# Metaformer block on one core: VectorE's order at a group's scales, and weight loads one per convolution group

## Chip, cores and metric

One core of one Trainium2 chip. The metric is the device time of a run in microseconds; a run is compared by the median.

## What is computed

```python
def reference(x, conv_weight, W1, b1, W2, b2):       # x: (16, 192, 32, 32)
    w_sym = mean of the four rotations of conv_weight (7 x 7, depthwise)
    x = x + dwconv(ln_c(x), w_sym)                   # ln_c: over the channels, eps 1e-6
    t = x as (16, 1024, 192)
    h = quantize(ln_t(t) @ sign(W1 - mean).T + b1)   # 768 hidden, groupwise
    out = quantize(gelu(h) @ sign(W2 - mean).T + b2)
    return t + out
# 5 groups of 3 images: gamma = max|group|; quantize = clip(y * 128 / (gamma + 1e-5)); image 16 keeps t alone
```

The quantisation needs the largest magnitude of a whole group of three images before any of its elements can go on, twice: once before the GELU, once before the output.

## The kernel before

**Convolution.** 48 groups of 4 channels (`conv_group`, L976) are products of TensorE with band matrices. Each group's band is fetched by four DMAs of 112 KB (`load_bands`, L296), two on SyncE's and two on ScalarE's queue, into three buffers up to group 25 and four from group 26 on (`BUFS`). A buffer is free when the group that used it last is done, so a band's fetch begins when the group three (later four) before it is done. VectorE adds each group's result to x (L750, one per group). POOL clears the fourth buffer (L406) once group 23 is done (`ROOM[FOURTH]`) and then, once 24 groups are done, starts ten DMAs that load the weights of the two linear layers: W1 (L409) and W2 (L411), five each, of 115 KB. VectorE reads them at groups 28 to 32 (`weight_sums`), and the signs and transposes of the weights follow. The region that they land in is part of the normalised input of the convolution, so it is free only once the groups that read it are done.

**Tokens.** An item is a half image, 512 tokens; there are 30 with a feed-forward part (`FT`), in groups of 6 (`GT`). The loop runs over steps s, and every engine has the instructions of several items in a step, in an order that is written out: hidden products for item s, GELU for s - 6 (`LAGA`), f16 high part and cast for s - 7 (`LAGH`), second products (`lower`, `upper`) for s - 8, largest output for s - 9, output for s - 15 (`LAGF`). f32 values go to TensorE as an f16 high part and an f16 remainder ("low part").

TensorE in a step: for each of six blocks of 128 hidden channels the products of item s (L1026 to L1028) and those of item s - 8 (L1058); after block 1 the transposes of tokens s + 1 (L1012, L1015), which need their normalisation; after block 4 the transposes of x for the output (`x_back`, L999 to L1004), which need the output of the item before (`fin`); at the end the upper products (L1068). The first product of step s + 1 needs the tokens' low parts.

VectorE in a step: `normal(s + 2)` (L816, four instructions), `high` (cast, L831), `final` (output, L897 and L898), `largest(s - 1)` (L844, of 3072 columns), `token_low(s + 1)` (L822, L824), `largest2` (L870). POOL has most of the hidden low parts (L435); from item 23 (`LAST`) VectorE has some of them (`low`, L839).

A group's scale: VectorE reduces the largest over the group (L847), TensorE turns it to a row (`as_row`, L1033), VectorE takes the row's maximum (`over_row`, L851), TensorE sends it to all partitions (`to_all`, L1038), VectorE works out the scale (`scale`, L856 to L866). This is at steps 6, 12, ..., 30 (`first`). The second scale (L879 to L887, `scale2`) does the same at steps 15, 21, ..., 39 (`first2`). There `to_all` on TensorE stands behind the transposes of tokens.

SyncE in a step fetches parked x (L341) for `normal`, and stores the output of item s - 16 (L348) once it is done; one queue does both in order.

## Time and profile before

| | |
|---|---|
| median of 3 runs | 613.7 us (611.32 to 615.29) |
| profiled execution, its time | 617.74 us |
| its span | 615.9 us |
| mean granted clock of TensorE | 0.918 |
| TensorE, VectorE, ScalarE, POOL busy | 81%, 76%, 62%, 36% |

The profile is of one execution; times are us from the start of its span, and L numbers are lines of the kernel before. Convolution runs from 88 to 235 us, tokens from there to the end. Idle time of an engine counts only where another one waits for it.

### The profile page before, as it was taken

The page shows a single profiled execution, that of the slowest core. Times are in us where ns is not written, and L with a number is a line of the kernel's source. Part 1 is how long each engine was busy: PE and PEld are TensorE (multiplying, and loading weights), DVE is VectorE, ACT ScalarE, POOL GpSimd, SP SyncE. Part 2 cuts the span into 40 slices and gives each one's busy share as a digit, 9 for nine tenths or more (in the row PEclk, how much of TensorE's full clock was granted, in tenths as well). Part 3 has the DMA queues.
Part 4 walks back from the last instruction along what each step waited for, and adds up shares of the span by engine and source line. Part 5 has one row for each costly group of instructions (what it writes and reads, how often), then busy time and mean ns, then how long its engine had stood idle before and what let it go on. Part 6 is the DMA issues. An engine that isn't in the chain of part 4 may idle for free.

```text
span 615.9 us, 9847 instructions
## 1 busy us (share of the span) xinstructions
PE 496.8 (81%) x3552; PEld 353.5 (57%) x3552; DVE 467.1 (76%) x1041; ACT 382.0 (62%) x598; POOL 219.7 (36%) x221
## 2 busy tenths in 40 slices
PE   2355527999969996758789989998999999987893
PEld 2255527999969995324335545555555555545562
DVE  7987861222228987996799898799989989699675
ACT  2688950000000353637799989998999898989550
POOL 4000000000400002212076747576666567558450
PEclk9666759999979997979999989999999999999798
DMA  8998325566965646940011000122222423263345
GB/s 223 290 316 248 104 61 150 149 175 169 204 161 150 178 124 250 386 157 1 27 51 53 27 27 0 52 82 74 78 74 77 133 78 101 80 230 104 125 135 178
DMA packets 55280, 81.29 MB, mean 132 GB/s; under 512 B 7361, under 2 KB 39105, under 8 KB 55232
## 3 DMA queue, kind: packets, MB, share of 16 engines
q1 hardware_dynamic: 39616, 68.28, 36.5%
q10 hardware_dynamic: 15136, 11.22, 6.5%
q0 software_dynamic: 480, 1.17, 0.9%
q8 instruction: 28, 0.46, 0.3%
q14 instruction: 20, 0.16, 0.1%
HBM read 53.12 MB, written 27.53 MB: 131 GB/s over the span
## 4 chain that ended last, share of the span: by engine, by line
PE 42%; DVE 22%; ACT 18%; DMA 10%; issue 5%; SPq 3%; ACTq 0%; DVEq 0%
PE bank L976 19%; DMA arena<-x 6%; PE bank L1058 5%; ACT arena L566 5%; DVE am L844 5%; ACT arena L560 4%; DMA arena<-kz_d 3%; PE bank L1026 3%; PE bank L1027 3%; PE bank L1028 3%; PE bank L1068 2%; DVE arena L816 2%; DVE arena L831 2%; ACT arena L482 2%; DVE arena L766 2%
## 5 line engine op out<-in xcount | busy, mean ns | idle before, releaser
L435 POOL TENSOR_TENSOR arena<-arena 128x512 f16<-128x512 f32 x159 | 186.9, 1212 | 120.6 <-DVE arena L831 99.3
L976 PE MATMUL bank<-arena 128*128 128x112 f32 (+1 forms) x1152 | 136.1, 283 | 20.8 <-ACT arena L482 12.6
L560 ACT ACTIVATE arena<-bank,b1s 128x512 f32<-128x512 f32 x180 | 125.1, 703 | 42.2 <-PE bank L1028 41.8
L976 PEld LDWEIGHTS bank<-arena 128*128 128x128 f32 x1152 | 135.0, 199 | 21.7 <-ACT arena L482 12.8
L1058 PE MATMUL bank<-arena 128*128 128x512 f16 x360 | 106.4, 390 | 5.4 <-ACT arena L584 3.6
L566 ACT ACTIVATE arena<-arena,gm 128x1024 f32<-128x1024 f32 x90 | 102.7, 1163 | 1.7 <-DVE gm L866 1.7
L844 DVE TENSOR_REDUCE am<-arena 128x1 f32<-128x3072 f32 x30 | 100.3, 3343 | 3.5 <-ACT arena L560 3.5
L750 DVE TENSOR_TENSOR arena<-bank,arena 128x512 f32<-128x512 f32 x48 | 33.2, 691 | 81.0 <-PE bank L976 80.9
L1026 PE MATMUL bank<-arena 128*128 128x512 f16 x180 | 71.0, 395 | 26.0 <-DVE arena L824 17.7
L497 ACT ACTIVATE arena<-arena,wmean 51x576 f16<-51x576 f32 (+1 forms) x10 | 8.6, 856 | 129.0 <-DVE wmean L724 116.2
L1027 PE MATMUL bank<-arena 128*128 128x512 f16 x180 | 70.6, 392 | 0.0
L1028 PE MATMUL bank<-arena 128*128 128x512 f16 x180 | 70.2, 390 | 0.0
L958 PE MATMUL bank<-identf,arena 128*128 128x128 f32 x128 | 33.4, 365 | 40.9 <-DMA arena<-x 40.9
L1058 PEld LDWEIGHTS bank<-arena 128*128 128x128 f16 x360 | 34.5, 99 | 47.7 <-issue 4.6
L426 POOL TENSOR_SCALAR arena<-arena,VR,SM 128x192 f32<-128x192 f32 x28 | 14.4, 526 | 108.8 <-DVE arena L816 75.7
L816 DVE TENSOR_SCALAR arena<-arena,VR,SM 128x192 f32<-128x192 f32 x92 | 44.1, 539 | 8.4 <-issue 8.2
L1026 PEld LDWEIGHTS bank<-arena 128*128 128x128 f16 x180 | 17.8, 99 | 56.6 <-DVE arena L824 21.3
L958 PEld LDWEIGHTS bank<-identf,arena 128*128 128x128 f32 x128 | 22.7, 194 | 42.8 <-DMA arena<-x 32.6
L831 DVE CAST arena<-arena 128x2048 f16<-128x2048 f32 (+1 forms) x30 | 35.8, 1195 | 13.6 <-ACT arena L566 11.9
L1068 PE MATMUL bank<-arena 128*64 128x256 f16 x720 | 46.1, 276 | 0.0
L1068 PEld LDWEIGHTS bank<-arena 128*64 128x64 f16 x720 | 37.5, 109 | 13.8 <-issue 13.4
L573 ACT ACTIVATE arena<-arena 128x1024 f16<-128x1024 f32 x37 | 39.7, 1072 | 1.7 <-PE bank L1068 1.7
(118 smaller groups left out, 684.9 us busy)
## 6 DMA issues: line engine op xcount, KB each, us to landing
arena<-park_d SPq DMA_DIRECT2D x44, 384.0 KB, 3.6
arena<-kz_d SPq DMA_DIRECT2D x100, 112.0 KB, 2.9
arena<-kz_d ACTq DMA_DIRECT2D x92, 112.0 KB, 3.4
park_d<-arena SPq DMA_DIRECT2D x6, 1536.0 KB, 14.5
arena<-x SPq DMA_DIRECT2D x8, 1024.0 KB, 8.9
out<-arena SPq DMA_DIRECT2D x32, 256.0 KB, 2.0
kz_d<-arena SPq DMA_DIRECT2D x8, 672.0 KB, 11.0
arena<-x SPq DMA_DIRECT2D x16, 256.0 KB, 9.8
```

The source lines that it names most:

```text
L435: last = pool.tensor_tensor(out=low_half(u, m, m + 1), in0=yslot(u)[:, 2 * m:2 * m + 2, :], in1=hib(u, m, m + 1), op=ALU.subtract)
L560: act.activation(yslot(s)[:, 2 * m:2 * m + 2, :], m1p[c % 2][:, :].rearrange("p (h n) -> p h n", h=2), ACT.Identity, bias=b1s[:, m:m + 1], ...
L566: act.activation(y, y, ACT.Gelu, scale=gm[:, 5:6]).then_inc(gelu, 1)
L816: last = v.tensor_scalar(TN[:, h % 2, jj, :], x1[:, jj, :], VR[:, n:n + 1], SM[:, n:n + 1], ALU.mult, ALU.add)
L844: v.tensor_reduce(am[:, u % GT:u % GT + 1], yslot(u), AX.XY, ALU.max, apply_absolute_value=True).then_inc(amx, 1)
L958: t.transpose(o[:, b, 0:P], nat[k % 2][:, b, cols], identf[:, :])
L976: last = t.matmul(ps[:, :, lo:hi], WB[BUFS[g]][:, 1 - db, c, :], xn[:, :, lo + db:hi + db], start=(db == 0), stop=(db == -1))
L1026: t.matmul(o, W1A[:, fs], TT[:, s % 2, 0, :], start=True, stop=False)
L1027: t.matmul(o, W1M[:, fs], TT[:, s % 2, 1, :], start=False, stop=False)
L1028: t.matmul(o, W1Q[:, fs], TT[:, s % 2, 2, :], start=False, stop=True).then_inc(mm1, 1)
L1058: last = t.matmul(o, W2T[:, m, 0:P], src, start=(i == n == 0), stop=(i == MT - 1 and n == 1))
L1068: last = t.matmul(m2b[e * C1:(e + 1) * C1, 0:QTR], W2T[:, m, P:C], src[:, e, :], start=(m == n == 0), stop=(m == MT - 1 and n == 1))
```

## The change

The weight loads go out one at a time: W1's five when 12, 13, ..., 16 convolution groups are done (`ROOM_W`), W2's five at 17 to 21, ahead of the clearing of the fourth buffer. Two assertions state that the region is free by then.

On VectorE: at steps 6, 12, 18 and 24 `token_low` comes directly behind `scale`, ahead of `normal`. At steps 15, 21 and 27 `over_row` comes ahead of `high`, and `scale2` and `final` ahead of `largest`. At step 33 `over_row` comes ahead of the cast, and `scale2` and `final` ahead of the low parts. All other steps keep their order, and no instruction is added or taken out.

```diff
+ROOM_W = (12, 17)
...
             pool.wait_ge(conv, ROOM[THIRD])
             pool.memset(WF[2], 0.0).then_inc(blank, 1)
+            for q in range(GROUPS):
+                pool.wait_ge(conv, ROOM_W[0] + q)
+                pool.dma_start(w1w[0:RP1, q, :], w1[q * 3 * RP1:(q + 1) * 3 * RP1, :]
+                               .rearrange("(p r) c -> p (r c)", r=3)).then_inc(ld_w, 16)
+            for q in range(GROUPS):
+                pool.wait_ge(conv, ROOM_W[1] + q)
+                pool.dma_start(w2w[0:RP2, q, :], w2[q * RP2:(q + 1) * RP2, :]).then_inc(ld_w, 16)
             pool.wait_ge(conv, ROOM[FOURTH])
             pool.memset(WF[3], 0.0).then_inc(blank, 1)
-            pool.wait_ge(conv, ROOM[FOURTH] + 1)
-            for q in range(GROUPS):
-                pool.dma_start(w1w[0:RP1, q, :], w1[q * 3 * RP1:(q + 1) * 3 * RP1, :]
-                               .rearrange("(p r) c -> p (r c)", r=3)).then_inc(ld_w, 16)
-                pool.dma_start(w2w[0:RP2, q, :], w2[q * RP2:(q + 1) * RP2, :]).then_inc(ld_w, 16)
...
-                if u >= LAST:
-                    dve.wait_ge(hiV, u + 1)
-                    low(u, HL, MT)
-                    dve.wait_ge(hiA, u + 1)
-                    low(u, LP, HL)
+                if u == LAST:
+                    lows_here(u)
...
+                if s <= FT:
+                    if first:
+                        if 0 <= s - LAGF < FT:
+                            final(s - LAGF)
+                        largest(s - 1)
+                        over_row(0, g)
+                        if s == FT:
+                            scale(g)
+                        if 0 <= s - LAGH < FT:
+                            high(s - LAGH)
+                        if s < FT:
+                            scale(g)
+                            token_low(s + 1)
+                    if s > 5 and s + 2 < FT:
+                        normal(s + 2)
+                    if first2:
+                        over_row(1, g2)
+                    if not first and 0 <= s - LAGH < FT:
+                        high(s - LAGH)
+                    if first2:
+                        scale2(g2)
+                    if not first and 0 <= s - LAGF < FT:
+                        final(s - LAGF)
+                    if not first and 1 <= s:
+                        largest(s - 1)
+                    if not first and 0 <= s + 1 < FT:
+                        token_low(s + 1)
+                else:
+                    if first2:
+                        over_row(1, g2)
+                    elif 0 <= s - LAGF < FT:
+                        final(s - LAGF)
                     if 0 <= s - LAGH < FT:
                         high(s - LAGH)
...
+                    if first2:
+                        scale2(g2)
+                        final(s - LAGF)
+                    if 0 <= s - LAGH < FT:
+                        lows_here(s - LAGH)
```

The order of VectorE's instructions at step 12, from a group's scale on, before (`arena` holds all big tiles, `gm` the scales, `bank` is PSUM):

```order
L866 TENSOR_SCALAR gm<-gm 128x1 [waits gelu,gsc_t]
L816 TENSOR_SCALAR arena<-arena,VR,SM 128x192 [waits trQ,ld_l2,nm]
L816 TENSOR_SCALAR arena<-arena,VR,SM 128x192 x3
L822 TENSOR_TENSOR arena<-bank,arena 128x512 [waits thi]
L824 TENSOR_TENSOR arena<-bank,arena 64x512 [waits tlo]
L870 TENSOR_REDUCE am<-arena 128x1 [waits ev2]
```

and after:

```order
L874 TENSOR_SCALAR gm<-gm 128x1 [waits gelu,gsc_t]
L827 TENSOR_TENSOR arena<-bank,arena 128x512 [waits thi]
L829 TENSOR_TENSOR arena<-bank,arena 64x512 [waits tlo]
L821 TENSOR_SCALAR arena<-arena,VR,SM 128x192 [waits trQ,ld_l2,nm]
L821 TENSOR_SCALAR arena<-arena,VR,SM 128x192 x3
L878 TENSOR_REDUCE am<-arena 128x1 [waits ev2]
```

The two low-part instructions, which take a bank and write 512 columns, have moved ahead of the four of the normalisation (128x192).

VectorE at step 15, before, from the cast on:

```order
L831 CAST arena<-arena 128x2048 [waits mm2b,gelu]
L851 TENSOR_REDUCE gs<-bank 1x1 [waits gtr1]
L844 TENSOR_REDUCE am<-arena 128x1 [waits ev1]
L879 TENSOR_SCALAR gm<-bank 128x1 [waits gall2]
L880 RECIPROCAL gm<-bank 128x1
L882 RECIPROCAL gm<-gm 128x1 [waits gsc2_t]
L884 TENSOR_SCALAR gm<-gm 128x1 [waits gsc2_t]
L887 TENSOR_SCALAR gm<-gm 128x1 [waits gsc2_t]
L897 SCALAR_TENSOR_TENSOR arena<-arena,gm,bank 128x512 [waits xps,gsc2]
L898 SCALAR_TENSOR_TENSOR arena<-arena,gm,bank 128x256
L822 TENSOR_TENSOR arena<-bank,arena 128x512 [waits thi]
L824 TENSOR_TENSOR arena<-bank,arena 64x512 [waits tlo]
```

and after:

```order
L859 TENSOR_REDUCE gs<-bank 1x1 [waits gtr1]
L836 CAST arena<-arena 128x2048 [waits mm2b,gelu]
L887 TENSOR_SCALAR gm<-bank 128x1 [waits gall2]
L888 RECIPROCAL gm<-bank 128x1
L890 RECIPROCAL gm<-gm 128x1 [waits gsc2_t]
L892 TENSOR_SCALAR gm<-gm 128x1 [waits gsc2_t]
L895 TENSOR_SCALAR gm<-gm 128x1 [waits gsc2_t]
L905 SCALAR_TENSOR_TENSOR arena<-arena,gm,bank 128x512 [waits xps,gsc2]
L906 SCALAR_TENSOR_TENSOR arena<-arena,gm,bank 128x256
L852 TENSOR_REDUCE am<-arena 128x1 [waits ev1]
L827 TENSOR_TENSOR arena<-bank,arena 128x512 [waits thi]
L829 TENSOR_TENSOR arena<-bank,arena 64x512 [waits tlo]
```

The row's maximum (`gs<-bank`) is now ahead of the cast, and the second scale and the output (128x512 and 128x256, which write `arena` from `gm` and `bank`) are ahead of the maximum of 3072 columns (`am<-arena`).

VectorE at step 33, before, from the cast on:

```order
L831 CAST arena<-arena 128x1024 [waits mm2b,gelu]
L839 TENSOR_TENSOR arena<-arena 128x1024 [waits hiV]
L839 TENSOR_TENSOR arena<-arena 128x512 [waits hiA]
L851 TENSOR_REDUCE gs<-bank 1x1 [waits gtr1]
L879 TENSOR_SCALAR gm<-bank 128x1 [waits gall2]
L880 RECIPROCAL gm<-bank 128x1
L882 RECIPROCAL gm<-gm 128x1 [waits gsc2_t]
L884 TENSOR_SCALAR gm<-gm 128x1 [waits gsc2_t]
L887 TENSOR_SCALAR gm<-gm 128x1 [waits gsc2_t]
L897 SCALAR_TENSOR_TENSOR arena<-arena,gm,bank 128x512 [waits xps,gsc2]
L898 SCALAR_TENSOR_TENSOR arena<-arena,gm,bank 128x256
L870 TENSOR_REDUCE am<-arena 128x1 [waits ev2]
```

and after:

```order
L859 TENSOR_REDUCE gs<-bank 1x1 [waits gtr1]
L836 CAST arena<-arena 128x1024 [waits mm2b,gelu]
L887 TENSOR_SCALAR gm<-bank 128x1 [waits gall2]
L888 RECIPROCAL gm<-bank 128x1
L890 RECIPROCAL gm<-gm 128x1 [waits gsc2_t]
L892 TENSOR_SCALAR gm<-gm 128x1 [waits gsc2_t]
L895 TENSOR_SCALAR gm<-gm 128x1 [waits gsc2_t]
L905 SCALAR_TENSOR_TENSOR arena<-arena,gm,bank 128x512 [waits xps,gsc2]
L906 SCALAR_TENSOR_TENSOR arena<-arena,gm,bank 128x256
L847 TENSOR_TENSOR arena<-arena 128x1024 [waits hiV]
L847 TENSOR_TENSOR arena<-arena 128x512 [waits hiA]
L878 TENSOR_REDUCE am<-arena 128x1 [waits ev2]
```

The low parts (128x1024 and 128x512) have moved from behind the cast to behind the output.

## Rows read from the trace of the kernel before

**Rows 1.** The page's first part: busy time and share of span

```profile
PE 496.8 (81%) x3552; PEld 353.5 (57%) x3552; DVE 467.1 (76%) x1041; ACT 382.0 (62%) x598; POOL 219.7 (36%) x221
```

**Rows 2.** Waits of TensorE, 357 to 560 us: total, times, longest

```profile
PE bank L1026 <- DVE arena L824: 5.6, 3, 2.4
PE bank L1033 <- DVE gm L847: 2.2, 2, 1.4
PE bank L999 <- DVE arena L898: 1.7, 2, 0.9
PE bank L999 <- issue: 1.4, 1, 1.4
```

**Rows 3.** Windows: length, busy PE, PEld, DVE, ACT, POOL; clock, DMA share, GB/s

```profile
120.00:136.00 16.00, 16.00 (x146) 16.00 (x145) 4.07 (x7) 0.00 (x0) 0.00 (x0) 1.00 0.64 172
...
168.00:176.00 8.00, 3.09 (x25) 2.97 (x26) 1.36 (x2) 0.00 (x0) 0.00 (x0) 0.87 1.02 219
176.00:184.00 8.00, 8.00 (x52) 8.00 (x53) 2.40 (x4) 0.00 (x0) 0.00 (x0) 0.70 0.36 109
```

**Rows 4.** Timeline of VectorE (start us, length us): additions of groups 26, 28, 29

```profile
167.98 0.69 DVE L750 TENSOR_TENSOR arena<-bank,arena 128x512 f32<-128x512 f32 x1 [1.99 <-PE bank L976]
...
181.12 0.69 DVE L750 TENSOR_TENSOR arena<-bank,arena 128x512 f32<-128x512 f32 x1 [9.22 <-PE bank L976]
...
183.80 0.69 DVE L750 TENSOR_TENSOR arena<-bank,arena 128x512 f32<-128x512 f32 x1 [0.48 <-PE bank L976]
```

**Rows 5.** Chain of waits, 155 to 200 us

```profile
163.25 12.42 DMA arena<-kz_d
```

**Rows 6.** DMA queues, 150 to 190 us: packets, MB, share

```profile
q0 software_dynamic: 480, 1.17, 14.2%
```

**Rows 7.** DMA issues, 104 to 158 us: count, KB, us to landing

```profile
arena<-kz_d ACTq DMA_DIRECT2D x39, 112.0 KB, 3.1
arena<-kz_d SPq DMA_DIRECT2D x38, 112.0 KB, 2.9
```

**Rows 8.** The same, 158 to 165 and 163 to 170 us

```profile
arena<-kz_d ACTq DMA_DIRECT2D x7, 112.0 KB, 5.4
...
arena<-kz_d SPq DMA_DIRECT2D x6, 112.0 KB, 8.4
```

**Rows 9.** Timeline of VectorE, step 12: normalisation

```profile
360.14 3.99 DVE L816 TENSOR_SCALAR arena<-arena,VR,SM 128x192 f32<-128x192 f32 x4
```

**Rows 10.** Timeline of TensorE, end of step 12, start of 13

```profile
361.53 1.53 PE L1068 MATMUL bank<-arena 128*64 128x256 f16 x24
365.50 0.61 PE L1026 MATMUL bank<-arena 128*128 128x512 f16 x1 [2.44 <-DVE arena L824]
```

**Rows 11.** Timeline of ScalarE, the same place

```profile
362.35 3.22 ACT L566 ACTIVATE arena<-arena,gm 128x1024 f32<-128x1024 f32 x3
367.00 0.69 ACT L560 ACTIVATE arena<-bank,b1s 128x512 f32<-128x512 f32 x1 [1.43 <-PE bank L1028]
```

**Rows 12.** Timeline of VectorE, steps 15 and 16

```profile
388.78 3.33 DVE L844 TENSOR_REDUCE am<-arena 128x1 f32<-128x3072 f32 x1
...
399.14 1.25 DVE L816 TENSOR_SCALAR arena<-arena,VR,SM 128x192 f32<-128x192 f32 x4 [2.98 <-issue]
```

**Rows 13.** Timeline of TensorE, step 15: the broadcast

```profile
389.51 0.38 PE L1038 MATMUL bank<-gs,arena 1*128 1x1 f32 x2
```

**Rows 14.** Windows, as rows 3, around step 24

```profile
486.00:496.00 10.00, 8.43 (x64) 5.11 (x63) 9.86 (x18) 8.27 (x13) 6.82 (x6) 1.00 0.10 40
```

**Rows 15.** Timeline of VectorE, step 26

```profile
504.22 1.25 DVE L816 TENSOR_SCALAR arena<-arena,VR,SM 128x192 f32<-128x192 f32 x4 [1.54 <-issue]
```

**Rows 16.** Timeline of VectorE, step 33: low parts

```profile
567.18 2.91 DVE L839 TENSOR_TENSOR arena<-arena 128x1024 f16<-128x1024 f32 x2
```

**Rows 17.** Timeline of TensorE, step 33

```profile
570.31 0.58 PE L1038 MATMUL bank<-gs,arena 1*128 1x1 f32 x2 [3.01 <-DVE gs L851]
```

**Rows 18.** Windows, as rows 3, end of step 33

```profile
570.30:578.00 7.70, 7.69 (x43) 4.68 (x44) 3.87 (x10) 1.00 (x3) 1.89 (x2) 0.58 0.39 128
```

More of the change, by code:

```diff
@@ L131, in build @@
         assert at + GROUPS * HID <= XB + 6 * BLK
+        assert XB + WW + WTN + GROUPS * 3 * C <= XB + ROOM_W[0] * NN * CG
+        assert all(at + (q + 1) * HID <= XB + (ROOM_W[1] + q) * NN * CG for q in range(GROUPS))
         w1s = [w1w[:, g, 0:3 * C // 2].bitcast(F16).rearrange("p (r c) -> p r c", r=3) for g in range(GROUPS)]
@@ L831, in high, with lows_here @@
                 v.tensor_copy(hib(u, ha(u), MT), yslot(u)[:, 2 * ha(u):2 * MT, :]).then_inc(hiV, 1)
-                if u >= LAST:
-                    dve.wait_ge(hiV, u + 1)
-                    low(u, HL, MT)
-                    dve.wait_ge(hiA, u + 1)
-                    low(u, LP, HL)
+                if u == LAST:
+                    lows_here(u)
+            def lows_here(u):
+                dve.wait_ge(hiV, u + 1)
+                low(u, HL, MT)
+                dve.wait_ge(hiA, u + 1)
+                low(u, LP, HL)
             def low(u, m0, m1):
@@ L907, in _ @@
                 first, first2 = s % GT == 0 and 1 <= g <= FT // GT, (s - LAGF) % GT == 0 and 0 <= s - LAGF < FT
-                if first:
-                    if 0 <= s - LAGF < FT:
-                        final(s - LAGF)
-                    largest(s - 1)
-                    over_row(0, g)
-                    if s == FT:
-                        scale(g)
+                if s <= FT:
[20 more added lines that the diff above has]
+                    if not first and 0 <= s - LAGF < FT:
+                        final(s - LAGF)
+                    if not first and 1 <= s:
[7 more added lines that the diff above has]
+                        final(s - LAGF)
@@ L915, in _ @@
                     if 0 <= s - LAGH < FT:
                         high(s - LAGH)
-                    if s < FT:
-                        scale(g)
-                if s > FT and not first2 and 0 <= s - LAGF < FT:
-                    final(s - LAGF)
-                if s > 5 and s + 2 < FT:
-                    normal(s + 2)
-                if not first and 0 <= s - LAGH < FT:
-                    high(s - LAGH)
-                if first2:
-                    over_row(1, g2)
-                elif not first and s <= FT and 0 <= s - LAGF < FT:
-                    final(s - LAGF)
@@ L929, in _ @@
-                if not first and 1 <= s <= FT:
-                    largest(s - 1)
-                if first2:
-                    scale2(g2)
-                    final(s - LAGF)
-                if 0 <= s + 1 < FT:
-                    token_low(s + 1)
+                    if first2:
[3 more added lines that the diff above has]
+                        lows_here(s - LAGH)
                 for k in range(len(BATCH)):
```

## Prediction

> **What bounds the kernel now.** I read five views. The page's first part [rows 1] gives TensorE 496.8 of 615.9 us: the busiest engine, idle or slowed for only a fifth. So the question is where it is held, and whether that is where the change acts. The waits of TensorE in the token stage [rows 2] are short and few: three for the tokens' low parts (5.6 us), two for a group's maximum (2.2), three for an output that VectorE has not finished (1.7 and 1.4). The stretches of the convolution [rows 3] show a full engine at clock 1.00 from 120 to 136 us, 3.09 busy of 8 between 168 and 176, and then a full engine at 0.70. VectorE's additions, one per convolution group, mark the pace [rows 4], the chain of waits names what was late [rows 5], and the DMA views say why [rows 6 to 8].
>
> The profiled execution took 617.74 us, 615.9 of span and 1.8 around it. The median of the runs is 613.7, 4.0 lower. I sum against the profiled one and take the saving in us off the median.
>
> **Weight loads, one per convolution group.** Before, ten loads went out within 5 us, behind group 24. They are 1.17 MB and took 14.2% of 16 engines over 40 us [rows 6], which is 5.7 us of all engines. The bands that the convolution needs take 0.64 of the engines at full pace [rows 3], so 0.36 is free and the burst needs 5.7/0.36 = 16 us to drain. From 160 us that gives 176, and group 28's band did land at 175.7, 12.4 us after it was issued [rows 5]. The additions of groups 26 and 29 are at 167.98 and 183.80 [rows 4]: 15.8 us for three groups. A group takes 2.68 at the steady pace (2.0 of idle and 0.69 of work before each addition), so three are 8.0, and 7.8 us are lost. Of these 4.9 are idle time of TensorE between 168 and 176, the other 2.9 the clock at 0.70 behind it [rows 3]. (The Trainium skill, TensorE: Matmul & The Clock Gate, Part 1, has the clock halved when the array idles and calls the ramp less than 1% of a typical span. Left out for that, this term would be 4.9 and the whole sum 16.2; the row at 0.70 decides for counting it.)
>
> After, a load goes out at each of groups 12 to 21. One load is a tenth, 0.57 us of all engines, in a group's 2.68 x 0.36 = 0.96 us of free time, so nothing piles up. What hides it: with three buffers a band may be issued when the group three before it is done, and is needed two groups later, 5.4 us. Its second DMA goes out some 0.7 us late and lands 3.1 us after issue [rows 7], leaving about 1.6. A load that costs each band 0.6 us fits; if the cover is gone, each of ten groups pays. On POOL the clearing of the fourth buffer now stands behind the loads, but the last load waits for group 21 and the clearing for 23, and the sums that read the weights come at group 28. Bounds of the term: 0 (the lateness moves, below) to 7.8; I take 7.8. Since TensorE runs the convolution to its end and everything behind starts from there, this shifts all that follows.
>
> **Low parts directly behind a scale (steps 6, 12, 18, 24).** VectorE's normalisation of a later half took 3.99 us at step 12 and stood ahead of the two low-part instructions; TensorE waited 2.44 for them [rows 9, 10]. Now they run from 360.1 to about 361.5, and TensorE, done with the step before at 363.0 (361.53 + 1.5), goes on at once. The normalisation then ends at 365.5; the transposes that need it come about 2.2 us into TensorE's step, at 365.2, so it just covers. ScalarE is in its three GELU pieces until 365.5 [rows 11], where before it had to wait until 367.0 for TensorE: it gains 1.5 at once. Above the gap lies what the slow clock behind it cost: the product at 365.50 took 0.61 us, and some 3 us went at half speed, at most 1.4 of them for nothing. Bounds 1.5 and 3.8; I take the gap, 2.4. At step 6, which lies before the stretch of rows 2, I take 0: ScalarE has its GELUs in one piece there and no slack behind them. At steps 18 and 24 the other 5.6 - 2.4 = 3.2 us go.
>
> **Second scale and output ahead of cast and maximum (steps 15, 21, 27).** The maximum alone is 3.33 us [rows 12]. The output of the first half of a group came behind it, and TensorE waited 1.7 + 1.4 us for it in all [rows 2]. It now comes about 2.3 us sooner: 3.3 less some 0.9 in which VectorE waits for TensorE's broadcast, which is behind a transposition of tokens, ends at 389.9 and was hidden by the maximum [rows 13]. There is a second effect: SyncE stores an output before it fetches the next parked tokens, so the normalisation at 399.14 sat idle for 2.98 us [rows 12]. It comes about 1.9 sooner, and with it the next maximum, for which TensorE waited 0.8 at step 18 (one of the two of 2.2 us; the other is at step 30 and stays).
>
> Together steps 15 to 27 can give 3.2 + 0.8 + 3.1 = 7.1. I don't take it all. VectorE was busy 9.86 of 10 us around step 24, TensorE 8.43 [rows 14]: once TensorE's waits are gone, VectorE's lateness is next. The maximum now stands ahead of the low parts, which come about 1 us later in these three steps, where my dates leave 0 to 0.6; and a fetch that made VectorE wait 1.54 at step 26 [rows 15] is not moved. I charge 0.5 at step 21 and 1 and 0.7 at steps 24 to 27: 4.9 stay. Bounds 0 and 7.1.
>
> **The end (step 33).** Low parts of VectorE (567.18, 2.91 us) stand ahead of the row maximum, and TensorE waits 3.01 for it and then runs 570.3 to 578.0 at clock 0.58 [rows 16 to 18]. Now the row maximum comes first, at 567, then cast, scale and output to 569.9; low parts end at 572.8. TensorE's next transposition waits for the output, 569.9, so its step ends near 573.3 and not 577.8: 4.5 us. VectorE gains less: output and cast of step 34 come behind the low parts, 3.0 us sooner than before. ScalarE waits for TensorE's product, not for VectorE, and gains the 4.5; it sets the pace of the steps that follow, so VectorE catches up in part. Bounds 3.0 and 4.5; I take 4.0.
>
> **Sum.** 7.8 + 2.4 + 4.9 + 4.0 = 19.1 us. The profiled execution would be 598.6, the median 613.7 - 19.1 = 594.6; I say 595. Edits that cost nothing: the number of instructions and their shapes are the same on every engine.
>
> **Rivals.**
> VectorE takes over: steps 15 to 27 give nothing, the end 3.0. For it: its 9.86 of 10 us busy [rows 14] and the later low parts. Against it: VectorE's idle 2.98 goes at the same time. 7.8 + 2.4 + 3.0 = 13.2, 600.5 us.
>
> The lateness moves: each load delays a band by more than the 1.6 us of cover. For it: landing was already 5.4 us on ScalarE's queue while the burst began [rows 8], which would be 0.7 late, 7 us in ten groups, and 602; I put the case at half that, 0.5 each, 599.7. Against it: that row has several loads in flight, and later there is one at a time. (The Trainium skill, DMA: Bandwidth & Descriptors, Queues, rings and completion order, has each engine take turns between queues by packet; by that a band waits for its share of a single load, which agrees with 0.57, but it should also have spared group 28, which landed 12.4 us late, so I lean on the rows.)
>
> Both together: 613.7 - 2.4 - 3.0 - 0.3 = 608, within 1%.
>
> Slower: bands land during a load as they did at the height of the burst, 8.4 us after issue on SyncE's queue [rows 8]. Place: groups 12 to 22. Price: 8.4 - 3.1 - 1.6 = 3.7 us for each of ten, 37 - 19.1 = 18 more, 631.6 us. It decides from 1.9 us each, a landing of 6.6 us. Against it: this needs a backlog of several us, and each load leaves 0.4 us of free time behind it.
>
> More than forecast: all waits go, 7.8 + 3.8 + 7.1 + 4.5 = 23.2, 590.5.
>
> **How the numbers follow.** Forecast 0.60 (its own range 591 to 599), VectorE takes over 0.16, lateness moves 0.12, both 0.05, slower 0.04, more 0.03. Faster by over 1% (about what a measurement of this kernel can tell from no change) is 0.60 + 0.16 + 0.12 + 0.03 = 0.91, within it 0.05, slower 0.04. The range goes from all waits, 589, to both middle rivals with some to spare, 604.
>
> **What would show it.** Right: additions 2.68 us apart through groups 26 to 29, no clock below 1.00 there, band landings under 4.5 us at groups 12 to 22; no wait of TensorE for the low parts at steps 12, 18 and 24; the 3.01 us wait gone and clock near 1.00 at step 33. Wrong: waits of TensorE for band DMAs between groups 12 and 24 (second rival, or the slower one), or new waits for the low parts at steps 16, 22 and 28 that sum to over 2.2 us (first rival).

## The result and the profile after

| | median, range, runs |
|---|---|
| before, beside it | 613.16 us (611.32 to 615.29), 4 |
| after | 598.44 us (598.03 to 598.90), 4 |
| ratio after/before | 0.9719 [0.9681, 0.9758] |

The change saves 14.7 us by these medians, where 19 were forecast; 598.4 lies in the range of 589 to 604. The ratio on record, 0.9719, is not that of the two medians (0.976, which lies just outside its interval); it stands for 17.2 us. A second comparison of the same two kernels (`e5_after`, below) gave 17.7 us by medians and 18.9 by its ratio, 0.9693 [0.9643, 0.9743]. So the size is known to some 4 us, 15 to 19. One run of `e4_end`, of 616.08 us, fell into a slower state of the chip and is left out of its times. The profiled execution of after took 598.64 us, the one of before 617.74: 19.1 us apart, which is the sum of the prediction to the tenth. That agreement is partly luck, as the experiments show: two terms were too large and two too small, and the profile of before happened to be long in two places.

The page of after: span, busy time, and the group of VectorE's normalisation.

```profile
span 596.8 us, 9847 instructions
PE 492.4 (83%) x3552; PEld 350.2 (59%) x3552; DVE 463.5 (78%) x1041; ACT 380.4 (64%) x598; POOL 218.8 (37%) x221
L821 DVE TENSOR_SCALAR arena<-arena,VR,SM 128x192 f32<-128x192 f32 x92 | 44.1, 539 | 1.8 <-issue 1.6
```

TensorE is still the busiest engine; its busy time fell by 4.4 us though it runs the same 3552 instructions, because less of it runs at the low clock. VectorE's normalisation has an idle time of 1.8 us ahead of it; before it was 8.4.

**The convolution.** Stretches of after (columns as in [rows 3]: busy time and count of PE, PEld, DVE, ACT, POOL, then granted clock, DMA share, GB/s). The first four answer to [rows 3], the next two are the start of the token stage, the last two answer to [rows 14] and [rows 18].

```profile
120.00:136.00 16.00, 15.62 (x140) 15.47 (x139) 3.92 (x6) 0.00 (x0) 1.75 (x3) 1.00 0.67 178
136.00:152.00 16.00, 15.81 (x142) 15.66 (x142) 4.15 (x6) 0.00 (x0) 3.09 (x6) 1.00 0.83 208
168.00:176.00 8.00, 8.00 (x74) 8.00 (x74) 2.99 (x5) 0.00 (x0) 0.00 (x0) 1.00 0.65 176
176.00:184.00 8.00, 8.00 (x74) 8.00 (x73) 6.57 (x10) 0.00 (x0) 0.00 (x0) 1.00 0.65 171
233.00:239.00 6.00, 3.27 (x17) 2.82 (x18) 3.06 (x10) 2.50 (x6) 3.89 (x8) 0.59 1.02 392
239.00:245.00 6.00, 6.00 (x20) 3.14 (x18) 5.35 (x40) 1.81 (x3) 1.52 (x3) 0.56 1.03 398
476.00:486.00 10.00, 9.38 (x68) 5.35 (x67) 9.97 (x15) 8.72 (x14) 7.80 (x8) 1.00 0.01 5
549.50:557.80 8.30, 7.38 (x73) 4.75 (x73) 6.76 (x16) 7.70 (x10) 6.41 (x5) 1.00 0.18 52
```

From 168 to 184 TensorE is full at 1.00, where before it had 3.09 of 8 and then 0.70. VectorE's additions keep 2.68 us apart through groups 26 to 29, where [rows 4] had 15.8 us for three:

```profile
169.03 0.69 DVE L755 TENSOR_TENSOR arena<-bank,arena 128x512 f32<-128x512 f32 x1 [1.99 <-PE bank L995]
171.71 0.69 DVE L755 TENSOR_TENSOR arena<-bank,arena 128x512 f32<-128x512 f32 x1 [1.99 <-PE bank L995]
174.39 0.69 DVE L755 TENSOR_TENSOR arena<-bank,arena 128x512 f32<-128x512 f32 x1 [1.99 <-PE bank L995]
177.07 0.69 DVE L755 TENSOR_TENSOR arena<-bank,arena 128x512 f32<-128x512 f32 x1 [0.48 <-PE bank L995]
```

But the stretch from 120 to 152, full before, now has two small waits for bands, of 0.38 and 0.19 us; TensorE's timeline there (start, us, count; idle before it and what ended it):

```profile
114.15 13.62 PE L995 MATMUL bank<-arena 128*128 128x128 f32 x120 [0.36 <-DMA arena<-kz_d]
128.15 16.30 PE L995 MATMUL bank<-arena 128*128 128x128 f32 x144 [0.38 <-DMA arena<-kz_d]
144.65 43.10 PE L995 MATMUL bank<-arena 128*128 128x128 f32 x384 [0.19 <-DMA arena<-kz_d]
```

DMA issues of after from 128 to 155 us (count, KB each, median us to landing), for [rows 7]; five loads of W1 and five of W2 fall here:

```profile
arena<-kz_d SPq DMA_DIRECT2D x20, 112.0 KB, 3.3
arena<-kz_d ACTq DMA_DIRECT2D x20, 112.0 KB, 3.9
arena<-w POOLq DMA_DIRECT2D x5, 114.8 KB, 3.2
arena<-w POOLq DMA_DIRECT2D x5, 114.0 KB, 3.3
```

Bands land 3.3 us after issue on SyncE's queue and 3.9 on ScalarE's, where [rows 7] had 2.9 and 3.1: later by 0.4 and 0.8 us, less than the 1.6 us of cover. The wait of 0.38 us ends at 128.15, when the first of the ten loads is only being issued, and four of the five profiles with the loads behind group 24 have such a wait at the same group, of 0.38 to 0.56 us; that of 0.19 falls among the loads.

**The token stage.** TensorE's waits from 340 to 545 us, against [rows 2]. The 5.6 us for the low parts (L824 before, L829 now) and the 1.7 for an output (L898, now L906) have no row any more; of the two for a maximum (L847, now L855) the one at step 30 is left. New, but for one wait of 0.2 us in before, is the first row, for ScalarE's eviction of the hidden products:

```profile
PE bank L1045 <- ACT arena L565: 1.8, 4, 0.6
PE bank L1052 <- DVE gm L855: 1.4, 1, 1.4
```

Step 12 on VectorE, for [rows 9]: low parts first, normalisation behind them.

```profile
354.82 0.68 DVE L827 TENSOR_TENSOR arena<-bank,arena 128x512 f16<-128x512 f32 x1
355.54 0.68 DVE L829 TENSOR_TENSOR arena<-bank,arena 64x512 f16<-64x512 f32 x1
```

And on TensorE, for [rows 10]: the next step's first product at 357.67 waits for nothing, and the transposes of tokens behind the normalisation are not late. Two small waits are left in the step, 0.25 us for POOL and, behind the rows shown, 0.36 for ScalarE.

```profile
356.21 1.53 PE L1087 MATMUL bank<-arena 128*64 128x256 f16 x24
357.67 0.39 PE L1045 MATMUL bank<-arena 128*128 128x512 f16 x1
...
358.75 0.61 PE L1077 MATMUL bank<-arena 128*128 128x512 f16 x2 [0.25 <-POOL arena L440]
```

Step 15 on VectorE, for [rows 12]: TensorE's broadcast comes out uncovered by 0.72 us, the output is done before the maximum, and the normalisation has no idle time, where it had 2.98.

```profile
381.66 0.16 DVE L887 TENSOR_SCALAR gm<-bank 128x1 f32<-128x1 f32 x1 [0.72 <-PE bank L1057]
...
382.49 0.75 DVE L905 SCALAR_TENSOR_TENSOR arena<-arena,gm,bank 128x512 f32<-128x512 f32 x1
...
383.54 3.35 DVE L852 TENSOR_REDUCE am<-arena 128x1 f32<-128x3072 f32 x1
...
388.99 1.23 DVE L821 TENSOR_SCALAR arena<-arena,VR,SM 128x192 f32<-128x192 f32 x4
```

Step 33 on TensorE, for [rows 17 and 18]: the broadcast (L1057) waits for nothing, and the clock stays at 1.00 (last row of the stretches above). One step later a new wait stands, 1.49 us for the fetch of parked x.

```profile
552.34 0.38 PE L1057 MATMUL bank<-gs,arena 1*128 1x1 f32 x2
...
554.87 0.63 PE L1018 MATMUL bank<-identf,arena 128*128 128x128 f32 x4 [0.72 <-issue]
...
561.62 0.63 PE L1018 MATMUL bank<-identf,arena 128*128 128x128 f32 x4 [1.49 <-DMA arena<-park_d]
```

**Where the span's 19.1 us went in this pair.** Taking the start of each step's last upper products (L1068, now L1087) in both traces, after is ahead by 5.3 us up to step 12, 8.3 at 13, 9.3 at 15, 11.0 at 19, 12.0 at 21, 12.7 at 25, 14.3 at 27, 14.0 at 31, 19.8 at 33, 18.4 at 34, 19.3 at the end. So the convolution brought 5.3 (7.8 forecast; 0.6 of the 5.3 was there before its first product), step 12 3.0 (2.4), steps 15 to 27 6.0 (4.9), step 33 5.8 less the 1.4 of the new wait, of which 1.2 comes back a step later (4.0).

### The profile page after: what moved, and what is told of

Read it like the earlier page. It is cut to its first block, busy times and chain, and to the rows that moved or that the text cites. A ratio compares the mean times of both kernels' runs of the same rounds, so it can differ in the third digit from the quotient of the medians.

```text
span 596.8 us, 9847 instructions
## 1 busy us (share of the span) xinstructions
PE 492.4 (83%) x3552; PEld 350.2 (59%) x3552; DVE 463.5 (78%) x1041; ACT 380.4 (64%) x598; POOL 218.8 (37%) x221
## 4 chain that ended last, share of the span: by engine, by line
PE 52%; ACT 19%; DVE 12%; DMA 10%; issue 4%; SPq 1%; ACTq 0%; DVEq 0%
PE bank L995 18%; PE bank L1077 8%; ACT arena L571 5%; DMA arena<-x 5%; ACT arena L565 5%; PE bank L1045 5%; PE bank L1087 4%; PE bank L1047 4%; PE bank L1046 4%; DMA arena<-kz_d 4%; DVE am L852 3%; ACT arena L487 2%; ACT arena L578 2%; DVE arena L771 2%; PE bank L977 2%
## 5 line engine op out<-in xcount | busy, mean ns | idle before, releaser
L995 PE MATMUL bank<-arena 128*128 128x112 f32 (+1 forms) x1152 | 133.8, 279 | 20.4 <-ACT arena L487 16.0
L565 ACT ACTIVATE arena<-bank,b1s 128x512 f32<-128x512 f32 x180 | 125.0, 705 | 36.2 <-PE bank L1047 35.9
L995 PEld LDWEIGHTS bank<-arena 128*128 128x128 f32 x1152 | 132.5, 196 | 21.5 <-ACT arena L487 16.2
L1087 PE MATMUL bank<-arena 128*64 128x256 f16 x720 | 46.1, 276 | 0.0
L1087 PEld LDWEIGHTS bank<-arena 128*64 128x64 f16 x720 | 37.5, 109 | 13.8 <-issue 13.4
L836 DVE CAST arena<-arena 128x2048 f16<-128x2048 f32 (+1 forms) x30 | 34.5, 1149 | 7.9 <-ACT arena L571 7.1
```

Of the source, the lines that this page charges most:

```text
L565: act.activation(yslot(s)[:, 2 * m:2 * m + 2, :], m1p[c % 2][:, :].rearrange("p (h n) -> p h n", h=2), ACT.Identity, bias=b1s[:, m:m + 1], ...
L995: last = t.matmul(ps[:, :, lo:hi], WB[BUFS[g]][:, 1 - db, c, :], xn[:, :, lo + db:hi + db], start=(db == 0), stop=(db == -1))
L1087: last = t.matmul(m2b[e * C1:(e + 1) * C1, 0:QTR], W2T[:, m, P:C], src[:, e, :], start=(m == n == 0), stop=(m == MT - 1 and n == 1))
```

## The experiments

The theory was the prediction's: four gains that add up. The rivals were VectorE's lateness in the token stage and late bands in the convolution.

### Each part alone

Four kernels, each the kernel before with one part of the change, beside 21 runs of before (614.17 us, 609.50 to 617.95).

**The weight loads alone** (`e1_weights`):

```diff
+ROOM_W = (12, 17)
...
-            pool.wait_ge(conv, ROOM[FOURTH])
-            pool.memset(WF[3], 0.0).then_inc(blank, 1)
-            pool.wait_ge(conv, ROOM[FOURTH] + 1)
             for q in range(GROUPS):
+                pool.wait_ge(conv, ROOM_W[0] + q)
                 ...                         # W1's load q
+            for q in range(GROUPS):
+                pool.wait_ge(conv, ROOM_W[1] + q)
                 ...                         # W2's load q
+            pool.wait_ge(conv, ROOM[FOURTH])
+            pool.memset(WF[3], 0.0).then_inc(blank, 1)
```

> The kernel before with the weight loads moved alone, one per convolution group from 12 on. Theory (the burst made the gap of groups 26 to 29, and it closes): additions 2.68 us apart through groups 26 to 29, three or four small waits for bands of 0.2 to 0.4 us between groups 12 and 20, the convolution ends 6 to 7 us sooner, and the median falls by 6 us (4.5 to 7.5). Rival (the profiled execution of before had a longer gap than its other runs): the profile shows the same closed gap, but the median falls by 1.5 to 4 us only.

Measured 607.80 us (606.74 to 611.73), ratio 0.9897 [0.9864, 0.9930]: 6.4 us, as expected. TensorE's timeline has 30 groups, the fifth to the 34th, in one row:

```profile
102.84 80.94 PE L979 MATMUL bank<-arena 128*128 128x128 f32 x720 [1.48 <-DMA arena<-kz_d]
```

Behind its first 1.48 us no band is late in this execution, so ten spread loads need not cause a wait. (In other profiles small ones stand among them, see the lengths below.)

**Low parts behind the scale alone**, steps 6, 12, 18 and 24 (`e2_lows`):

```diff
                     if s < FT:
                         scale(g)
+                        token_low(s + 1)
...
-                if 0 <= s + 1 < FT:
+                if not first and 0 <= s + 1 < FT:
                     token_low(s + 1)
```

> The kernel before with the tokens' low parts directly behind the scale at steps 6, 12, 18 and 24 alone. Theory (TensorE's three waits for L824 are on the path): the wait of 2.44 at step 12 and the two of 1.57 go, the median falls by 4 us (2.4 at step 12 and about 0.8 each at 18 and 24, where VectorE is late next). Rival (VectorE's lateness returns at the outputs of steps 15, 21, 27, whose waits of 0.87, 0.87 and 1.43 grow by what was gained): the median falls by 2.4 or less.

Measured 610.38 us (606.18 to 613.80), 0.9936 [0.9902, 0.9970]: 3.8 us. TensorE's waits from 355 to 560 us:

```profile
PE bank L1000 <- DVE arena L898: 2.1, 2, 1.2
PE bank L1027 <- ACT arena L560: 1.8, 4, 0.6
```

The three waits for low parts are gone. In their place stand the waits for ScalarE's evictions (L560), seen in the whole change too, and the wait for the output at step 15 grew from 0.87 to 1.23 us. By steps: +3.0 at step 12, -0.4 at 15, -0.4 at 18, +0.7 at 19, +0.7 at 25, -0.3 at 27. Those at 18 and 27 prove nothing: `e1_weights`, unchanged there, has -0.6 and -0.2. The 0.4 at step 15 does not stand in it, so the rival, VectorE's lateness coming back at the outputs, holds in that small part.

**Second scale and output first alone**, steps 15, 21 and 27 (`e3_scale2`):

```diff
+                early2 = first2 and s < FT
+                if early2:
+                    over_row(1, g2)
                 if not first and 0 <= s - LAGH < FT:
                     high(s - LAGH)
-                if first2:
+                if early2:
+                    scale2(g2)
+                    final(s - LAGF)
+                elif first2:
                     over_row(1, g2)
...
-                if first2:
+                if first2 and not early2:
                     scale2(g2)
                     final(s - LAGF)
```

> The kernel before with the second scale and the output ahead of cast and maximum at steps 15, 21 and 27 alone (row maximum ahead of the cast, output ahead of the 3.3 us maximum). Theory: the three waits for the output (0.87, 0.87, 1.43) and the 0.81 for the maximum at step 18 go, the idle 2.98 of VectorE at step 16 shrinks to under 1.2, the median falls by 4 us (3 to 5). Rival (the low parts, now behind the maximum, are late): waits of TensorE for the low parts appear at steps 16, 22 and 28, and the median falls by under 2.

Measured 610.69 us (606.36 to 611.61), 0.9947 [0.9917, 0.9977]: 3.5 us. Waits of TensorE, 355 to 555 us:

```profile
PE bank L1032 <- DVE arena L824: 5.6, 3, 2.4
PE bank L1039 <- DVE gm L847: 1.4, 1, 1.4
```

The 5.6 us are those of before, in the same three places. The low parts that now come behind the maximum at steps 15, 21 and 27 are not late for TensorE. By steps: 1.06 at 15, 0.96 at 18, 1.06 at 21, 1.67 at 27, together 4.8 us, more than the medians give but inside their interval (1.4 to 5.1).

**Step 33 alone** (`e4_end`):

```diff
+                if s == 33:
+                    over_row(1, g2)
                 if not first and 0 <= s - LAGH < FT:
                     high(s - LAGH)              # without its low parts at s == 33
-                if first2:
+                if first2 and s != 33:
                     over_row(1, g2)
...
                 if first2:
                     scale2(g2)
                     final(s - LAGF)
+                if s == 33:
+                    lows_here(26)
```

> The kernel before with the second scale and the output ahead of the low parts at step 33 alone. Theory (a TensorE wait of 3.01 us and the half clock behind it): the wait goes, clock above 0.9 in that step, the median falls by 4.5 us (3.5 to 5.5). Rival (only the wait counts, and VectorE's later low parts take the rest): 2 to 3 us.

Measured 610.69 us (606.06 to 613.05), 0.9941 [0.9913, 0.9968]: 3.5 us, at the lower end of what was expected. The broadcast no longer waits, and the step looks as in the whole change:

```profile
564.58 0.38 PE L1045 MATMUL bank<-gs,arena 1*128 1x1 f32 x2
...
567.11 0.63 PE L1006 MATMUL bank<-identf,arena 128*128 128x128 f32 x4 [0.72 <-issue]
```

The four savings are 6.4 + 3.8 + 3.5 + 3.5 = 17.2 us, each known to some 2 us. They add up to what the whole brings (14.7 to 18.9), within some 4 us: no large part of one gain is another's.

### The whole again, and its neighbours

Four kernels, beside 11 runs of before (614.57 us, 610.71 to 619.32).

**The whole change, unchanged** (`e5_after`):

> The changed kernel once more, beside the next three on the same chip. Theory (the profiled execution of before was 3 to 4 us longer than its median by chance, in the clock behind step 33 and in the loads of x): the changed kernel is 15.5 us (14.5 to 17) under before's median here, and its runs differ by little. Rival (the 19.1 of the two spans is the true size): 18 us or more.

Measured 596.89 us (593.31 to 598.41, 6 runs), 0.9693 [0.9643, 0.9743]: 17.7 us, above the 14.5 to 17 that were expected and just under the 18 of the rival. The profiled execution of it and that of `e9_before` (below) have spans of 595.3 and 611.4 us. They are 16.1 apart, of which, taken as above, 3.8 us were there by step 12; step 12 brought 3.1, steps 15 to 27 5.5 and step 33 4.2. With the first comparison and the 17.2 of the parts, the change is worth some 15 to 19 us.

**Both loads of a pair behind each of groups 17 to 21**, instead of one behind each of 12 to 21 (`e6_pairs`):

```diff
             for q in range(GROUPS):
-                pool.wait_ge(conv, ROOM_W[0] + q)
+                pool.wait_ge(conv, ROOM_W[1] + q)
                 ...                         # W1's load q
-            for q in range(GROUPS):
-                pool.wait_ge(conv, ROOM_W[1] + q)
                 ...                         # W2's load q
```

> The changed kernel with two weight loads at each of groups 17 to 21 in place of one at each of 12 to 21. Theory (a group has about 1 us of free DMA time and 1.6 us of cover, a load takes 0.57): two loads, 1.14 us, leave a backlog of 0.1 to 0.2 us a group, which the cover takes: within 1 us of the changed kernel, band landings of 4 to 5 us. Rival (any second load in a group already makes its band late): waits of TensorE for bands of 0.5 us or more in five groups, and 3 to 6 us slower than the changed kernel.

Measured 596.58 us (595.65 to 598.42), 0.9703 [0.9662, 0.9745]: the same as the whole. Issues of bands from 139 to 153 us, while the ten loads go out, and TensorE's timeline at groups 20, 21 and 22:

```profile
arena<-kz_d SPq DMA_DIRECT2D x10, 112.0 KB, 3.8
arena<-kz_d ACTq DMA_DIRECT2D x10, 112.0 KB, 4.5
```

```profile
147.28 2.90 PE L993 MATMUL bank<-arena 128*128 128x128 f32 x24 [0.20 <-DMA arena<-kz_d]
150.48 2.90 PE L993 MATMUL bank<-arena 128*128 128x128 f32 x24 [0.30 <-DMA arena<-kz_d]
153.61 32.71 PE L993 MATMUL bank<-arena 128*128 128x128 f32 x288 [0.22 <-DMA arena<-kz_d]
```

Two loads per group make bands land later, 3.8 and 4.5 us after issue where one load gave 3.3 and 3.9, and three groups in a row now wait, for 0.7 us in all. That is close to the backlog of the theory, and it can't be seen in the time. The rival, 0.5 us or more in each of five groups, does not hold.

**The ten loads in one burst behind group 21**, the rest of the change kept (`e8_burst21`):

```diff
+            pool.wait_ge(conv, ROOM_W[1] + GROUPS - 1)
             for q in range(GROUPS):
-                pool.wait_ge(conv, ROOM_W[0] + q)
                 ...                         # W1's load q
-            for q in range(GROUPS):
-                pool.wait_ge(conv, ROOM_W[1] + q)
                 ...                         # W2's load q
```

> The changed kernel with all ten weight loads in one burst at group 21, three groups earlier than in the kernel before, in the stretch with three buffers. Theory (the loss is the backlog, not the place): a gap of TensorE of about 10 us over groups 23 to 26, larger than before's 5 us since the cover is 1.6 us and not one group more; 8 to 13 us slower than the changed kernel. Rival (the loss came from where the burst stood, beside the switch to four buffers): no gap over 2 us, within 3 us of the changed kernel.

Measured 603.79 us (601.39 to 605.74), 0.9816 [0.9772, 0.9861]: 6.9 us over the whole change, where 8 to 13 were expected. TensorE's timeline, then the two stretches behind the gap's start:

```profile
159.51 2.90 PE L993 MATMUL bank<-arena 128*128 128x128 f32 x24 [0.45 <-DMA arena<-kz_d]
167.10 29.75 PE L993 MATMUL bank<-arena 128*128 128x128 f32 x240 [4.69 <-DMA arena<-kz_d]
```

```profile
160.00:167.00 7.00, 2.41 (x22) 2.23 (x21) 0.69 (x1) 0.00 (x0) 0.83 (x5) 0.93 1.10 208
167.00:175.00 8.00, 7.89 (x46) 7.93 (x47) 0.69 (x1) 0.00 (x0) 0.00 (x0) 0.64 0.46 144
```

The gap is there again, ahead of group 24 where before it was ahead of group 28, with the low clock behind it: a wait of 4.69 us and 0.64, as against 4.64 and 0.70. The gap came out half of what I had expected from the smaller number of buffers at group 21. So it is the backlog of ten loads at once that costs the time; neither the place nor the number of buffers changed it much.

**Fetch of parked x ahead of the store**, for the new wait of 1.49 us at step 34 (`e7_fetch`):

```diff
-                    store(u, u % Y2R, st_o[u % Y2R])
                     if 2 * KEPT <= u < early[0] - 2:
                         bring_back(u + 2)
+                    store(u, u % Y2R, st_o[u % Y2R])
```

> The changed kernel with SyncE's fetch of a parked half image for the output put ahead of the store, in each step. Theory (the new wait of 1.49 us at step 34 is for a fetch that stands behind three store DMAs, 1.6 us of issue): that wait goes, and 0.8 us of time (0.3 to 1.5). Rival (ScalarE sets the pace there anyway, or the later store holds up the next fetch for the normalisation): the wait goes and the time stays within 0.3 us, or rises.

Measured 595.80 us (592.30 to 598.28), 0.9686 [0.9639, 0.9733]. The 1.1 us to the whole change can't be told from nothing in six runs. The wait for the fetch is gone and others stand there (0.92 for ScalarE, 0.56 for POOL). In `e5_after` the wait was only 0.60 us and in `e6_pairs` there was none, so it is not worth a change. Inconclusive, and small at best.

### The kernel before again, and one order more

Beside 7 runs of before (614.07 us, 609.74 to 617.15).

**The kernel before, once more with a profile** (`e9_before`):

> The kernel before once more, for a second profile. Theory (the first profile was long by chance at step 33): the wait of TensorE for the row maximum at step 33 is 2 to 3 us with a clock above 0.8 behind it, so that the step takes 2 to 3 us less than the 12.6 us of the first profile; the gap at groups 26 to 29 is there as before, 7 to 8 us. Rival (the first profile is typical): step 33 takes 12 us or more again.

One run, 613.27 us, span 611.4. TensorE's timeline around the gap, and the stretch at step 33:

```profile
155.71 13.62 PE L976 MATMUL bank<-arena 128*128 128x128 f32 x120 [0.43 <-DMA arena<-kz_d]
173.31 18.90 PE L976 MATMUL bank<-arena 128*128 128x128 f32 x144 [3.98 <-DMA arena<-kz_d]
```

```profile
565.70:573.00 7.30, 5.80 (x38) 3.78 (x40) 5.30 (x12) 3.02 (x4) 3.38 (x3) 0.77 0.22 64
```

The gap behind the burst belongs to the kernel (a wait of 3.98 us here, 4.64 in the first profile). So do small waits for bands such as the 0.43: the first profile of before merely had none from 120 to 152 us. The slow clock at step 33 varies: 0.77 here, 0.58 there. The wait for the row maximum was 3.65 us and the step took 11.0, 1.6 less than in the first profile where the theory had 2 to 3 less: that one was long by chance, but by less than I thought.

**After, with low parts ahead of the maximum at steps 15, 21 and 27** (`e10_low_first`):

```diff
+                    if first2 and 0 <= s + 1 < FT:
+                        token_low(s + 1)
                     if not first and 1 <= s:
                         largest(s - 1)
-                    if not first and 0 <= s + 1 < FT:
+                    if not first and not first2 and 0 <= s + 1 < FT:
                         token_low(s + 1)
```

> The changed kernel with the tokens' low parts put ahead of the maximum at steps 15, 21 and 27. Theory (the charge of 2.2 us in the forecast for VectorE's later low parts was wrong, since TensorE waits for none of them): within 1 us of the changed kernel, steps 15, 21 and 27 end within 0.2 us of where they did. Rival (they hold TensorE up without showing as a wait): 1 to 2 us faster.

Measured 597.69 us (596.03 to 600.62, 4 runs), 0.9715 [0.9671, 0.9759]: no better. Measured from its step 12, steps 15, 21 and 27 of this profile end when they did in after, so there was no lateness of the low parts to remove, and step 18 gains 0.4 instead of 0.96, since the wait for a maximum is back (two waits, 1.8 us, where after has one of 1.4):

```profile
PE bank L1054 <- DVE gm L855: 1.8, 2, 1.4
```

Its step 33 took 9.7 us all the same: the row maximum is not what TensorE waits for there, but ScalarE for 1.59 us, with a clock of 0.82 over the step.

### Lengths over all profiles

Two lengths, read from TensorE's timeline of each profile in the same way. The convolution is taken from the first L976 product to the first transposition of the second weight (L1078 before), step 33 from one step's last upper products to the next's. A burst puts all ten loads behind one group.

| | convolution, us | step 33, us |
|---|---|---|
| ten loads behind group 24, step 33 as before: before, `e9_before`, `e2_lows`, `e3_scale2` | 147.5, 147.5, 147.8, 147.4 | 12.6, 11.0, 9.8, 9.2 |
| the same loads, step 33 changed: `e4_end` | 147.9 | 6.8 |
| loads spread, step 33 as before: `e1_weights` | 138.1 | 9.8 |
| loads spread, step 33 changed: after, `e5_after`, `e6_pairs`, `e7_fetch`, `e10_low_first` | 141.4, 142.1, 141.9, 142.3, 141.6 | 6.8, 6.8, 6.8, 7.7, 9.7 |
| ten loads behind group 21, step 33 changed: `e8_burst21` | 151.5 | 7.7 |

With the loads behind group 24 the convolution takes 147.6 us (five profiles), with them spread in the whole change 141.9 (five): 5.7 us less. Step 33 takes 10.4 us without its change (mean of five profiles) and 7.4 with it (seven, the odd 9.7 included): 3.0 us less.

Where the 5.7 us come from is seen in VectorE's additions, one per group, which are 2.68 us apart at the steady pace. Additions 26 to 29 [rows 4] lose 7.8 us against that pace in before, and 6.6, 6.7, 6.8 and 7.2 in the other four profiles with the loads behind group 24: 7.0 on average. With the loads spread they lose nothing, in all six. In `e8_burst21` it is additions 23 to 26, which lose 7.6. Its convolution is longer than that of before by 3.9 us, but not by the gap: 2.7 us of that are lost ahead of addition 12, where no load is out, and 1.4 between 12 and 23.

From addition 12 to 23, where the spread loads go out, the five profiles of the whole change lose 0.4 to 2.1 us (mean 1.1) and `e1_weights` 0.1; of the five with the loads behind group 24 four lose nothing and one 1.6 (mean 0.3). So spreading costs some 0.8 us there, if it is more than chance. Ahead of addition 12 no load is out in any profile, and they still differ by up to 4.4 us there.

From the end of the convolution to step 8 the burst kernels take 87.4 to 87.8 us, those with spread loads 87.8 to 89.7, about 1.2 us more: TensorE's first work on tokens ran at 0.59 and 0.56 from 233 to 245 us in after. Before has the same a little later, though (0.50 from 241 to 247 us), and the DMA engines are full in both stretches (1.02 and 1.03 of their share). What makes the 1.2 us is open.

## Why the prediction was right, and where its terms were not

**Weight loads: mechanism right, size too large.** Forecast 7.8, typical 5.7 and some 1.2 given back behind it, so 4.5. The steps "nothing piles up" and "a load that costs each band 0.6 us fits" held in the main: landing 3.3 and 3.9 us with one load per group, no wait in `e1_weights`, and 0.7 us of waits with two loads per group. By its letter the sign "waits of TensorE for band DMAs between groups 12 and 24" did appear in after, but with 0.38 and 0.19 us where the second rival needs 5. What failed is taking 7.8 us from one execution. It was the largest loss of the five profiles of such a burst (mean 7.0). Nor is all of it gained: where the loads now go out, some 0.8 us more are lost, and ahead of them chance took 0.4 more (7.0 - 0.8 - 0.4 is the 5.7, but for rounding). The 9.4 us of `e1_weights` (138.1 against 147.5) are this 7.8 with nothing lost among the loads, and 1.7 that it was ahead before the first load went out, which is luck. "This shifts all that follows" was not quite so either: the start of the token stage gives a little back.

**Low parts behind the scale: step 12 mis-sized low, 18 and 24 high.** At step 12 3.0 us came, 2.4 were taken out of bounds of 1.5 to 3.8; the slow clock behind the gap, which I had left out, accounts for what is above: TensorE ran at 0.50 from 365.5 to 368.5 in before, which cost 1.5 us, and after has new waits of 0.25 and 0.36 us there. The normalisation "just covers", as worked out. Step 6 gave nothing, as forecast. At steps 18 and 24 I took both waits of 1.6 us to go in full. Instead TensorE now waits 0.62 us for ScalarE a little later, with smaller waits beside it, and 0.7 us were gained at each. The timeline of ScalarE in after shows why:

```profile
417.75 3.22 ACT L571 ACTIVATE arena<-arena,gm 128x1024 f32<-128x1024 f32 x3
420.87 0.68 ACT L565 ACTIVATE arena<-bank,b1s 128x512 f32<-128x512 f32 x1
```

```profile
423.49 0.39 PE L1045 MATMUL bank<-arena 128*128 128x512 f16 x1 [0.62 <-ACT arena L565]
```

Three GELUs in one piece hold back the evictions (L565) that free TensorE's banks. ScalarE is what is late next there, and the prediction looked at it only for steps 6 and 12.

**Second scale and output first: too small, for a wrong reason.** The gain was right in kind: outputs on time, the idle 2.98 us of the normalisation gone, the maximum of step 18 on time (0.96 for 0.8). The charge of 0.5 + 1 + 0.7 us for VectorE's lateness was wrong. VectorE is busy 9.97 of 10 us from 476 to 486, yet `e3_scale2` has no new wait for low parts, and `e10_low_first`, which would have removed one, gains nothing. A full VectorE was not a late one here. The error of 2.2 us down and that of 1.8 us up at steps 18 and 24 nearly cancel; together with outputs worth more than their waits, 6.0 us came for 4.9.

**The end: right, near the lower bound.** 4.0 forecast within 3.0 to 4.5. The single step gave 5.8 us in the profiled pair, but 3.0 as a mean over profiles, because the first profile of before was the longest there; `e4_end` alone gave 3.5 by the medians.

**The sum.** 5.7 - 1.2 + 3.0 + 6.0 + 3.0 = 16.5 us is what the profiles make typical, between the measured 14.7 and 17.7, and close to the 16.1 of the second pair of profiles. Forecast 19.1: the 2.6 too many are mostly the weight term, sized from a single execution.

**The rivals.** VectorE takes over (600.5): refuted as a mechanism, though its number is not far off. Lateness moves, and slower: refuted at their size by landing times and by `e6_pairs`; what is left of the lateness is under 1 us. All waits go: not so, ScalarE's and the fetch's take the place of some. The time alone could not have told these apart: 598.4 is nearer to both middle rivals (599.7 and 600.5) than to the 595 of the forecast.

Two of the rivals' sums don't follow from their own terms. Half of 0.7 us is 0.35 and not the 0.5 that was put in (which gives 599.6), and with that 0.5 for each of ten loads the weight term keeps 2.8 us, not 0.3, so that both rivals together come to 605.5 and not 608. Neither touches the forecast.

## What to carry to other kernels

A burst of bulk loads beside transfers that pace an engine costs more than its bytes: it makes a gap, and the gap a slow clock. Spread over a stage with free DMA share, at one or even two loads per unit of work, the same bytes cost under 1 us. At a step where a scale is worked out, the short instructions that others wait for belong directly behind it, and long reductions and casts behind these; but look at every engine for what is late next, ScalarE's long pieces included. A term read from one gap in one profile needs a second profile of the same kernel, to see which small waits come and go.

## What I had not expected of the hardware

The low clock behind a wait varies from run to run with the same instructions: step 33 of kernels without its change took 9.2 to 12.6 us, with a granted clock of 0.77 in one profile of before and 0.58 in the other. That makes one profile's price of such a wait uncertain by some 2 us. (The Trainium skill, TensorE: Matmul & The Clock Gate, Part 1, says that the cost of the warm-up varies from run to run, which these rows bear out, and puts it below 1% of a typical span. Here a single one, the 3 us between 12.6 and 9.8 at step 33, is half a per cent, and there are two such places.)

Low parts on VectorE (L847, two instructions) took 1.99 us at step 33 in after and 2.91 in before [rows 16], and the four normalisation instructions 3.79 us at step 12 but 1.23 at step 15. For the normalisation the traces show what goes with it. Of its 92 instructions in after, the 62 with no GpSimd instruction beside them took 0.36 to 0.38 us each; the 18 that had one beside them throughout took 0.38 to 1.38, with a median of 1.21 (in before 64 and 17, with the same medians). No run changed GpSimd's work alone, so the cause is not shown. (The Trainium skill, SBUF — State Buffer, SBUF: two separate sides, has an exclusive port pair that VectorE and GpSimd share: a VectorE instruction in a two-port mode or with two SBUF inputs and one of GpSimd block each other for their whole length. These durations fit that; whether the normalisation runs in such a mode no run here shows.)
